# Four graph layers on one core: nodes without edges first, and their dense work beside the edges' tiles

## The chip, the core and the metric

The kernel runs on one core of one Trainium2 chip. The metric is the device time of one execution in microseconds (us). Five engines have programs of their own: TensorE (PE in the profile, its weight loads PEld), VectorE (DVE), ScalarE (ACT), GpSimd (POOL) and SyncE (SP), which only issues DMAs. They meet by semaphores.

## The reference, cut to what matters

There are 10000 nodes with rows of 512 f32, and 5000 edges (src, dst) with drawn ends, sorted by dst. So at least half of the nodes receive no edge.

```python
h = x + segment_sum(x[src], dst)                       # GIN
x = layernorm(x + relu(h @ W1 + b1) @ W2 + b2)

mean = segment_sum(x[src], dst) / max(count, 1)        # SAGE and batch norm
h = mean @ W_l.T + b_l + x @ W_r.T
x = layernorm(x + relu(batch_norm(h)) + x)

# GAT twice (4 heads of 256 columns, every node has a loop edge), then a dense layer
h1 = relu(gat_conv(x,  src+loop, dst+loop, W1, ...))   # softmax over a node's edges
h2 = relu(gat_conv(h1, src+loop, dst+loop, W2, ...))
x = layernorm(x + h2 @ Wfc + bfc)

xw = x @ W.T                                           # GCN and batch norm
h = segment_sum(norm[:, None] * xw[row], col) + b      # loops included
x = layernorm(x + gelu(batch_norm(h)) + x)
```

What counts for the change: a node without an edge takes nothing from another node. Its sum is zero, its softmax is the loop's own weight, 1, and its GCN row is its own row times its scale.

## The kernel before, in words

**Tiling.** Nodes lie in DRAM in 20 groups of 512 (`GROUP`), each of 4 subtiles (`S`) of 128 rows (`P`). Edges lie in 40 tiles of 128 (`T`). An edge stage gathers the source rows of a tile by one indirect DMA on POOL, multiplies them on PE by a 128x128 matrix that joins edges of one target, and stores the 128 sums in a table in DRAM (`sum`, or `sum_gat` with the attention's weights). Sums that cross a tile's edge are joined at the end, in "rim" rows. A node stage takes the sum of each of its nodes out of that table by an indirect DMA per subtile on POOL, through `slot_i` (`gather_sums`, L1639); nodes without an edge find a row of zeros. Products in f32 are made of three in f16, of high and low parts (`split_product`, L316 to L327).

**Stages.** The program is a list of stages. In each, every engine has its own list of work in a fixed order, written out by hand; no planner sets it. Between two stages there is a barrier (all engines drain and meet at a semaphore, in `Kernel.run`, L287 to L292). In order: setup (degrees, slots and masks of the edges) with the first edge sum; `gin_stage` (L1644); `edge_product_stage` (L1086: sums of the x1 rows times W_l); `sage_stage` (L1843); batch norm coefficients; `batch_norm_stage` (L2040, which also makes h1 = x W1 of the first attention with its score columns); `edge_attention_stage` for h1 (L1249); `gat_middle_stage` (L2298: sums, bias and ReLU, times W2, stores h2); `edge_attention_stage` for h2; `gat_stage` (L2483: sums, bias and ReLU, times Wfc, residual and norm, stores x3); `edge_sum_stage` over x3 (L975); `gcn_stage` (L2738); coefficients; `output_stage` (L2858).

**An attention tile.** POOL gathers a score row of the target and a full row (1028 values and more) of the source. DVE adds the scores (L1367) and leaks them, ACT spreads them to 128 columns, PE turns them into rows (L1543, a product with the identity), DVE masks them and takes the maximum (L1380, L1385) and subtracts it, ACT takes the exponential, PE sums the weights (L1552), DVE inverts (L1401) and makes four 128x128 matrices (`a_lhs`, L1414), PE multiplies them by the gathered rows (L1560), ACT evacuates the two banks and SP stores them. Most buffers of this chain, its PSUM banks too, are double or more.

**GIN.** Per group SP loads x, POOL gathers the sums and adds the bias (L1732), DVE and ACT make high and low parts, PE multiplies twice, POOL does a part of the norm (L1617), DVE applies it, and SP stores the group's 512 rows of x1 with one contiguous DMA (`store`, L1703). In `output_stage` POOL makes the norm's shift (L2908, L2911) and SP stores the group's output rows with one contiguous DMA (L2896).

**SAGE and GCN.** Per group SP loads the rows, POOL gathers sums, PE transposes both by 128x128 blocks (`tp`, L1986 and L2838) and multiplies them, columns of features being the partitions. SAGE's POOL also gathers 40 single scales of 4 bytes. `Held` (L2715) is the class that finds room in SBUF for the GCN rows that stay there until the output.

Of the kernel before, what the change touches and what calls it, by code (L numbers as in the profile page):

```python
# [5 lines left out]
F32 = mybir.dt.float32  # L6
# [7 lines left out]
P = 128  # L14
# [35 lines left out]
class Dims:  # L50
    def __init__(self, nodes, edges):
# [10 lines left out]
        self.slots = self.none + 1  # L62
        self.last_real = nodes - (self.groups - 1) * GROUP
        assert self.sent >= nodes and 0 < self.last_real <= GROUP
# [107 lines left out]
class Kernel:  # L172
    def __init__(self, nc, ctx, dims, dram):
# [25 lines left out]

        self.apart = sb("apart", [P, T, P], F16)  # L200
        self.dst_f = sb("dst_f", [P, T + 1], F32)
        self.src_i = sb("src_i", [P, T], I32)
        self.dst_logits_i = sb("dst_logits_i", [P, T], I32)
        self.src_dinv_i = sb("src_dinv_i", [P, T], I32)
        self.slot_i = sb("slot_i", [P, d.blocks], I32)
        self.mean_scale = sb("mean_scale", [P, T], F32)
        self.src_dinv = sb("src_dinv", [P, T], F32)
        self.src_dinv_neg = sb("src_dinv_neg", [P, T], F32)
        self.rim_mean_scale = sb("rim_mean_scale", [P, 1], F32)

        self.dst_dinv = sb("dst_dinv", [P, T], F32)
        self.rim_dinv = sb("rim_dinv", [P, 1], F32)
        self.node_scale = sb("node_scale", [P, d.blocks], F32)
        self.rim_cross = sb("rim_cross", [P, T], F32)
        self.rim_pen = sb("rim_pen", [P, T], F32)
        self.rim_tiles = sb("rim_tiles", [P, 1], F32)
        self.node_dinv = sb("node_dinv", [P, d.blocks], F32)
# [135 lines left out]
class Tables:  # L353


    def __init__(self, kn):
# [6 lines left out]
        self.degrees = take("target_degrees", 2)  # L363


def setup_stage(kn, mem, tables):
# [20 lines left out]
    blank = sb("blank", [1, HC], F32)  # L387
# [47 lines left out]
    off_first = sb("off_first", [P, T, T], F16)  # L435
# [13 lines left out]
    rim_count_ps = kn.bank[0][0:T, 0:1]  # L449

# [6 lines left out]
    consts = Steps(take("const_steps", 13))  # L457
# [4 lines left out]
    products = take("setup_products", 7)  # L462
    COUNTED, ROWS_SUMMED, BASED, TIED, SORTED_DONE, ENDS_DONE, RIM_COUNTED = range(1, 8)
# [3 lines left out]
    turned = take("turned", Q)  # L467
# [9 lines left out]
    edge_steps = Steps(take("edge_steps", 6))  # L477
# [4 lines left out]
    mask_steps = Steps(take("mask_steps", 12))  # L482
    slot_steps = Steps(take("slot_steps", 14))
# [14 lines left out]
    def sync_late(sp):  # L498
        sp.wait_ge(degrees.sem, degrees.at(2))
        sp.dma_start(dram["dinv"].rearrange("(p r) c -> p (r c)", p=P), kn.node_dinv[:]).then_inc(dinv_out.sem, 16)  # L500
        sp.wait_ge(dinv_out.sem, dinv_out.at(16))
        sp.wait_ge(tables.zeroed.sem, tables.zeroed.at(48))

    def gpsimd(pool):
# [5 lines left out]
        g.memset(blank[:], 0.0).then_inc(blank_ready.sem, 1)  # L510
# [6 lines left out]
        g.memset(kn.eps[:], EPS)  # L517
        b = st.mark(g.memset(kn.minus_half[:], -0.5))
# [13 lines left out]
        assert n == st.sig.at(13)  # L532

        pool.wait_ge(hist_ready.sem, hist_ready.at(1))
        g.tensor_scalar(degree[:], hist[:], 1.0, None, ALU.add).then_inc(degrees.sem, 1)
        pool.wait_ge(degrees.sem, degrees.at(1))
        g.tensor_tensor(kn.node_dinv[:], degree[:], kn.minus_half[:], ALU.pow).then_inc(degrees.sem, 1)

    def scalar(act):
# [3 lines left out]
        for c in range(Q):  # L543
            act.wait_ge(turned.sem, turned.at(c + 1))
            act.copy(high_turned[0:K, c * 4 * P:(c + 1) * 4 * P], wide_ps[c % 2][0:K, :]).then_inc(turned_ready.sem, 1)

    def vector(dve):
# [30 lines left out]
        dve.wait_ge(consts.sig.sem, consts.sig.at(13))  # L578
# [81 lines left out]
        dve.wait_ge(consts.sig.sem, consts.sig.at(13))  # L660
# [17 lines left out]
    def ends(dve):  # L678
# [10 lines left out]
        v.tensor_tensor(off_first[:], dst.unsqueeze(2).broadcast_to([P, T, T]),  # L689
# [11 lines left out]
    def finish(dve):  # L701
# [5 lines left out]
        st.mark(v.tensor_scalar(kn.dst_logits_i[:], kn.dst_f[:, 0:T], float(GAT_ROW // LOGITS), None, ALU.mult))  # L707
        edge_steps.mark(v.scalar_tensor_tensor(out=kn.src_dinv_i[:], in0=edge_f[:, :, 2], scalar=float(K),
                                               in1=edge_f[:, :, 0], op0=ALU.mult, op1=ALU.add))
# [2358 lines left out]
```

## Time and profile before

| what | value |
|---|---|
| median of 3 runs (lowest, highest) | 3914.8 us (3913.59, 3915.11) |
| profiled execution, time | 3912.85 us |
| profiled execution, span | 3911.1 us |
| mean granted TensorE clock over the span | 0.932 |
| PE busy | 3419.3 us, 87% of the span, 19416 matmuls |
| DVE busy | 2155.2 us, 55% |
| ACT busy | 1463.1 us, 37% |
| POOL busy | 1452.1 us, 37% |
| DMA | 821 MB, mean 210 GB/s |

The stages, read from the barriers in the trace:

| stretch, us | stage |
|---|---|
| 0 to 199.2 | setup and the first edge sum |
| 199.3 to 655.4 | GIN |
| 659.7 to 835 | edge products |
| 835.2 to 1128 | SAGE |
| 1137 to 1624.5 | batch norm and h1 |
| 1628 to 1812.5 | edge attention over h1 |
| 1812.9 to 2688.7 | middle attention stage |
| 2688.7 to 2873.5 | edge attention over h2 |
| 2873.8 to 3401.5 | second attention's nodes, dense layer |
| 3402.5 to 3495.8 | edge sum over x3 |
| 3495.8 to 3758 | GCN |
| 3763.6 to 3911.1 | output |

The span is the time from the first to the last record of the profiled execution; its own time is 1.75 us longer. Shares of busy time are means over stages with different limits, so each stage is read by itself. The granted clock is told as a share of full speed, 1.00 being 2.4 GHz. In a row, "128x512 f32<-128x344 f16" is the shape and type of what is written and read, and the text in brackets at the end of a row is the time in which the engine was idle ahead of it and what ended that.

### The profile page before, as it was taken

What the parts mean: (1) busy time and instruction counts of PE and PEld (TensorE: products, weight loads), DVE (VectorE), ACT (ScalarE), POOL (GpSimd) and SP (SyncE); (2) the same over time, 40 slices, a digit from 0 to 9 for tenths busy, and PEclk for the clock granted to TensorE, in tenths of its full rate; (3) what the DMA queues carried; (4) which work ended last, traced back from release to release, by engine and by line L of the source; (5) the groups of instructions that cost most, each with busy time, mean ns of one, the idle gap of its engine ahead of it and who ended that gap; (6) DMA issues with size and microseconds to landing.
All of it is one profiled execution on the core that took longest, in us unless ns stands there. A gap on an engine that the chain in (4) does not pass through costs nothing. (4 is left out here: it accounts for less than half of the span.)

```text
span 3911.1 us, 55988 instructions
## 1 busy us (share of the span) xinstructions
PE 3419.3 (87%) x19416; PEld 2074.1 (53%) x19416; DVE 2155.2 (55%) x3972; ACT 1463.1 (37%) x2580; POOL 1452.1 (37%) x1231
## 2 busy tenths in 40 slices
PE   4669998989969999886999999998859999859964
PEld 3234443545637666664666666666635555315543
DVE  7257775845554444276543443413758888406667
ACT  1323332533324444353332332322534444233357
POOL 2345553225422222253333323212536666343312
PEclk7789999989979999997999999999979999979976
DMA  2667774656659999597978878944957777375558
GB/s 82 201 184 198 196 201 146 201 172 228 227 195 259 279 274 281 180 280 213 256 192 204 204 194 198 200 119 146 280 209 259 262 261 262 123 231 186 174 167 275
DMA packets 624227, 821.41 MB, mean 210 GB/s; under 512 B 378374, under 2 KB 378374, under 8 KB 622032
## 3 DMA queue, kind: packets, MB, share of 16 engines
q1 hardware_dynamic: 556880, 598.37, 50.3%
q0 software_dynamic: 67200, 221.25, 20.1%
q8 instruction: 71, 1.16, 0.1%
q14 instruction: 76, 0.62, 0.1%
HBM read 470.83 MB, written 263.59 MB: 188 GB/s over the span
## 5 line engine op out<-in xcount | busy, mean ns | idle before, releaser
L326 PE MATMUL bank<-w_lo,t_r_hi 128*128 128x344 f16 (+1 forms) x2560 | 838.8, 328 | 0.0
L327 PE MATMUL bank<-w_hi,t_r_hi 128*128 128x344 f16 (+1 forms) x2560 | 838.6, 328 | 0.0
L325 PE MATMUL bank<-w_hi,w_lo 128*128 128x344 f16 (+1 forms) x2240 | 716.7, 320 | 49.8 <-DMA w_lo<-g_row_lo 31.3
L2415 DVE SCALAR_TENSOR_TENSOR t_z<-w_lo,t_z 128x256 f32<-128x256 f32 x320 | 243.5, 819 | 396.4 <-DMA w_lo<-h 393.4
L326 PE MATMUL bank<-w_lo,w_hi 128*128 128x344 f16 (+1 forms) x1280 | 419.6, 328 | 0.0
L327 PE MATMUL bank<-w_hi 128*128 128x344 f16 (+1 forms) x1280 | 419.4, 328 | 0.0
L2389 POOL TENSOR_TENSOR t_row_lo<-t_r,t_row_hi 128x1024 f16<-128x1024 f32 x80 | 174.9, 2187 | 509.8 <-ACT t_row_hi L2436 509.8
L327 PEld LDWEIGHTS bank<-w_hi,t_r_hi 128*128 128x128 f16 x2560 | 250.9, 98 | 168.8 <-issue 0.8
L326 PEld LDWEIGHTS bank<-w_lo,t_r_hi 128*128 128x128 f16 x2560 | 250.9, 98 | 162.5 <-issue 0.6
L325 PE MATMUL bank<-w_hi 128*128 128x344 f16 x960 | 298.3, 311 | 21.8 <-DMA w_hi<-t_row_lo 19.2
L325 PEld LDWEIGHTS bank<-w_hi,w_lo 128*128 128x128 f16 x2240 | 219.3, 98 | 181.7 <-issue 50.8
L325 PE MATMUL bank<-l_z_hi,w_lo 128*128 128x512 f16 x640 | 244.4, 382 | 1.4 <-DVE l_z_lo L2798 1.4
L326 PE MATMUL bank<-l_z_lo,w_hi 128*128 128x512 f16 x640 | 244.3, 382 | 0.0
L327 PE MATMUL bank<-l_z_hi,w_hi 128*128 128x512 f16 x640 | 244.1, 381 | 0.0
L325 PE MATMUL bank<-w_hi,t_r_lo 128*128 128x512 f16 x640 | 243.6, 381 | 0.0
L2591 POOL TENSOR_TENSOR t_r_lo<-t_r,t_r_hi 128x512 f16<-128x512 f32 x160 | 196.0, 1233 | 97.1 <-ACT t_r_hi L2659 90.1
L2447 ACT ACTIVATE w_hi<-bank 128x344 f32<-128x344 f32 x240 | 104.5, 454 | 339.5 <-PE bank L327 339.4
L2656 ACT ACTIVATE t_r<-bank,vec_scaled 128x512 f32<-128x512 f32 x160 | 109.6, 685 | 293.0 <-PE bank L2687 241.4
L1639 POOL DMA_INDIRECT t_z<-sum_gat,slot_i x160 | 163.0, 1019 | 122.0 <-SPq L292 79.1
L2243 ACT ACTIVATE b_wide<-bank 128x344 f32<-128x344 f32 x240 | 109.2, 456 | 253.1 <-PE bank L327 253.1
L1617 POOL TENSOR_TENSOR n_power<-n_moments,eps 128x4 f32<-128x4 f32 x80 | 15.9, 199 | 502.9 <-DVE n_moments L1611 502.9
L2622 DVE SCALAR_TENSOR_TENSOR t_z<-w_lo,t_z 128x256 f32<-128x256 f32 x320 | 187.0, 645 | 21.4 <-DMA t_z<-sum_gat,slot_i 13.3
(345 smaller groups left out, 6732.2 us busy)
## 6 DMA issues: line engine op xcount, KB each, us to landing
w_lo<-h SPq DMA_DIRECT2D x160, 512.0 KB, 5.7
h<-b_wide SPq DMA_DIRECT2D x80, 516.0 KB, 9.6
h<-w_hi SPq DMA_DIRECT2D x80, 516.0 KB, 2.9
sum_gat<-a_out SPq DMA_DIRECT2D x80, 514.0 KB
l_x<-x SPq DMA_DIRECT2D x40, 1024.0 KB, 9.1
sum<-e_out SPq DMA_DIRECT2D x120, 256.0 KB
g_x<-in_x SPq DMA_DIRECT2D x20, 1024.0 KB, 5.6
x<-g_y SPq DMA_DIRECT2D x20, 1024.0 KB, 5.1
```

The costliest lines, as they stand in the source:

```text
L325: pe.matmul(out, s_lo, m_hi, start=(k == 0), stop=False)
L326: pe.matmul(out, s_hi, m_lo, start=False, stop=False)
L327: mm = pe.matmul(out, s_hi, m_hi, start=False, stop=last)
L1617: self.nc.gpsimd.tensor_tensor(self.power[:, u, :], self.moments[:, u, :, 1], self.kn.eps[:], ALU.add)\
L1639: pool.indirect_dma_start(out, None, sums, bass.IndirectOffsetOnAxis(ap=kn.slot_i[:, g * S + s:g * S + s + 1], axis=0), bounds_check=kn.d. ...
L2243: act.activation(wide[s][:, n * THIRD:(n + 1) * THIRD], mm[n], ACT.Copy, scale=UNSCALE)\
L2389: nc.gpsimd.tensor_tensor(row_lo[:, s, :], r_f[s % 2][:], row_hi[:, s, :], ALU.subtract)\
L2415: ins = v.scalar_tensor_tensor(out=z[u][:, s, cols], in0=hrow[:, s, cols], scalar=z[u][:, s, HC + h:HC + h + 1], in1=z[u][:, s, cols], op0 ...
L2447: act.activation(wide[s % 2][:, third * THIRD:(third + 1) * THIRD], mm[s % 2][third], ACT.Copy, scale=UNSCALE).then_inc(wide_done.sem, 1)
L2591: g_.tensor_tensor(r_lo[:, u, k, :], r_f[k % 2][:], r_hi[:, u, k, :], ALU.subtract)\
L2622: ins = v.scalar_tensor_tensor(out=z[u][:, s, cols], in0=hrow[:, s, cols], scalar=z[u][:, s, HC + h:HC + h + 1], in1=z[u][:, s, cols], op0 ...
L2656: act.activation(r_f[k % 2][:], tp[k % 4][:], ACT.Relu, scale=A_SCALE, bias=kn.vec_scaled[:, bias + k:bias + k + 1]).then_inc(r_done.sem, 1)
```

## The change

**Order.** Setup also counts the nodes with no edge (`alone`), ranks them with two small products on PE, and gives every node a place: those without an edge first, the others behind them, each in their old order (`places_of_nodes`). `Dims.early` is the number of groups, a multiple of two, that are sure to hold only nodes without an edge: (10000 - 5000) // 1024 * 2. The input x keeps its order. `gin_stage` reads by nodes and stores x1 by places, with four indirect DMAs per group on POOL (`to_places`) in place of SP's one; all stages behind it work by places; `output_stage` stores by nodes again, with four indirect DMAs per group on POOL. A small DRAM table by node (scale and place) is read in GIN and SAGE, 40 times each, once per tile and end of the edges (`look_up`). A table by place (node, slot, scale) is written by 80 indirect DMAs on POOL in `edge_product_stage`, two per tile, and loaded by SP in `sage_stage`. There the `early` groups skip the gathers of sums, their transposes and the additions.

```diff
+        self.early = max(nodes - edges, 0) // (2 * GROUP) * 2
+def to_places(kn, pool, rows, g, s, landed):
+    pool.indirect_dma_start(kn.dram["x1"], bass.IndirectOffsetOnAxis(ap=kn.place_i[:, g * S + s:g * S + s + 1], axis=0),
+                            rows, None, bounds_check=kn.d.padded - 1, oob_is_err=False).then_inc(landed.sem, 16)
+def look_up(kn, pool, out, at, t, landed):
+    pool.indirect_dma_start(out[:, t, :], None, kn.dram["by_node"],
+                            bass.IndirectOffsetOnAxis(ap=at[:, t:t + 1], axis=0),
...
 def edge_product_stage
+        def store_by_place(k):
+            pool.indirect_dma_start(dram["by_place"], bass.IndirectOffsetOnAxis(ap=kn.place_at_i[:, k:k + 1], axis=0),
+                                    kn.by_place[:, k, :], None, ...)
...
 def gin_stage, gpsimd
             norm.pool(pool, *divmod(g, 2))
             if g + 3 < G:
                 load_sums(g + 3)
+            store(g)
+            for t in range(g * per, min((g + 1) * per, d.tiles)):
+                look_up(kn, pool, kn.src_by, kn.src_at_i, t, found)
...
 def sage_stage, gpsimd
+        pool.wait_ge(table_in.sem, table_in.at(16))
...
+        for t in range(T):
+            look_up(kn, pool, dst_by, kn.dst_at_i, t, found)
+        for g in range(E, G):
             load_sums(g)
...
 def output_stage, gpsimd
+            if g:
+                store(g - 1)
+        store(G - 1)
```

**Merged stages.** The work of an edge stage becomes a class with one method per engine and tile (`AttentionEdges`, `RowEdges`), and a new stage runs it beside the dense work of the first 8 groups. The edge steps are shared out evenly over the slots of that work: a slot is a third of a subtile's product in the first (96 slots for 45 steps), a subtile's product in the second and third (32 slots for 45 and for 41 steps). Each engine does a slot's dense work and then its edge steps, in a fixed order. Behind each stands the old node stage, now for the other 12 groups.

```diff
+def shared_out(steps, slots):
+    return [range(n * steps // slots, (n + 1) * steps // slots) for n in range(slots)]
...
+            for third in range(THIRDS):                  # gat_middle_early_stage, PE
+                pe.wait_ge(wide_done.sem, wide_done.at((j - 1) * THIRDS + third + 1))
+                split_product(pe, mm[third], ..., CH).then_inc(prod.sem, 1)
+                for e in steps[j * THIRDS + third]:
+                    edges.tensor_step(pe, e)
...
+            for s in range(S):                           # rows_product_early_stage, PE
+                if g + 1 < E:
+                    turn(g + 1, (2 * s, 2 * s + 1))
+                pe.wait_ge(y_done.sem, y_done.at(g * S + s - 1))
+                split_product(pe, mm[s % 2][:], ..., CH, hidden if s == 0 else None).then_inc(prod.sem, 1)
+                for e in steps[g * S + s]:
+                    edges.tensor_step(pe, e)
...
+    def tensor(self, pe, t):                             # AttentionEdges, one tile on PE
+        pe.wait_ge(self.lhs_ready.sem, self.lhs_ready.at(t + 1))
+        pe.wait_ge(self.evacuated.sem, self.evacuated.at(2 * t))
+        for h in range(HEADS):
+            ins = pe.matmul(...)
+        ins.then_inc(self.summed.sem, 1)
+        if t + 1 < self.T:
+            self.sum_weights(pe, t + 1)
+        if t + 2 < self.T:
+            self.score_rows(pe, t + 2)
+    def vector(self, dve, t):                            # and on DVE, as vector_step(dve, t - 1)
+        self.matrices(dve, t)
+        if t + 1 < self.T:
+            self.maxima(dve, t + 1)
...
-        kn.add(edge_attention_stage(kn, dram["h1"]))
+        kn.add(gat_middle_early_stage(kn))
         kn.add(gat_middle_stage(kn))
-        kn.add(edge_attention_stage(kn, dram["h2"]))
+        kn.add(rows_product_early_stage(kn))
         kn.add(gat_stage(kn, 2))
         with ExitStack() as mem:
-            kn.add(edge_sum_stage(kn, mem, dram["x3"], (kn.src_dinv, kn.src_dinv_neg), kn.dst_dinv, kn.rim_dinv))
-        with ExitStack() as mem:
             held = Held(kn, mem)
+            kn.add(gcn_early_stage(kn, held))
             kn.add(gcn_stage(kn, held))
```

To fit beside the dense work, `AttentionEdges` keeps 4 gathered tiles (6 before) and 3 outputs (4 before), and single buffers for the masked scores and `a_lhs`, and single banks for the totals, the score rows and the weights' sums. The score rows are now turned by `pe.transpose` in place of a product with the identity. In `gat_middle_early_stage` DVE makes `z * A_SCALE + bias` and the low part of 1024 columns for each subtile, ACT the high part, and both parts are transposed by DMAs from SP. In `rows_product_early_stage` the rows of h2 are transposed on PE, ACT makes ReLU and the high part of each of 8 chunks of 512 columns per group, and POOL the low part, behind whose first group the edges' first four tiles of gathers stand. `gcn_early_stage` keeps the edges' buffers in rows of `Held` that the GCN stage fills only later.

## Rows read from the trace of the kernel before

**Rows 1.** Stretches: stages. Columns: window, length, five engines busy, clock, DMA share, GB/s.

```profile
835.20:1128.00 292.80, 282.24 (x1600) 168.97 (x1600) 157.66 (x241) 94.34 (x160) 127.51 (x124) 0.97 0.63 212
1628.00:1812.50 184.50, 143.87 (x748) 111.26 (x748) 122.94 (x462) 84.12 (x201) 79.79 (x80) 0.92 0.78 233
1812.90:2688.70 875.80, 847.35 (x5776) 567.60 (x5776) 343.81 (x402) 259.92 (x401) 254.92 (x160) 0.98 0.79 192
2873.80:3401.50 527.70, 489.73 (x2560) 262.61 (x2560) 388.05 (x640) 202.87 (x320) 303.52 (x280) 0.96 0.65 239
3402.50:3495.80 93.30, 54.16 (x82) 16.85 (x82) 1.16 (x2) 42.51 (x80) 39.99 (x40) 0.79 0.72 228
```

**Rows 2.** Stretches: slices of 50 us inside the two attention node stages.

```profile
2000.00:2050.00 50.00, 50.00 (x345) 33.55 (x343) 20.93 (x25) 14.23 (x22) 13.86 (x9) 1.00 0.80 191
3000.00:3050.00 50.00, 50.00 (x265) 26.68 (x264) 40.74 (x67) 20.96 (x34) 31.74 (x30) 1.00 0.72 266
```

**Rows 3.** Order of instructions, PE and DVE, attention tile: start, us, engine, line.

```profile
1700.26 2.00 PE L1560 MATMUL bank<-a_rows,a_lhs 128*128 128x256 f32 x8 [0.42 <-DVE a_lhs L1414]
...
1702.53 1.14 PE L1543 MATMUL bank<-ident,a_spread 128*128 128x128 f32 x8
1704.09 2.00 PE L1560 MATMUL bank<-a_rows,a_lhs 128*128 128x256 f32 x8 [0.43 <-DVE a_lhs L1414]
...
1703.35 0.69 DVE L1414 SCALAR_TENSOR_TENSOR a_lhs<-apart,a_out 128x512 f32<-128x512 f16 x1
```

**Rows 4.** Order of instructions, PE, second attention's node stage: twelve transposes.

```profile
3008.65 1.47 PE L2687 MATMUL bank<-ident,t_z 128*128 128x128 f32 x12
3009.96 0.38 PE L325 MATMUL bank<-w_hi,t_r_lo 128*128 128x512 f16 x1
```

**Rows 5.** Line L325, PE: count, ns min/median/max, first and last start, us.

```profile
L325 PE MATMUL bank<-w_hi x960: 308/309/495, 1837.0 to 2642.1; 128*128 128x344 f16 x192
L325 PE MATMUL bank<-l_z_hi,w_lo x640: 378/379/635, 849.1 to 3756.9; 128*128 128x512 f16 x160
L325 PE MATMUL bank<-w_hi,t_r_lo x640: 378/379/632, 2911.5 to 3391.9; 128*128 128x512 f16 x160
L325 PE MATMUL bank<-w_hi,e_z_lo x160: 378/379/390, 674.5 to 826.0; 128*128 128x512 f16 x160
```

**Rows 6.** Groups by line: count | busy, mean | idle before, its end.

```profile
L2591 POOL TENSOR_TENSOR t_r_lo<-t_r,t_r_hi 128x512 f16<-128x512 f32 x160 | 196.0, 1233 | 97.1 <-ACT t_r_hi L2659 90.1
L1639 POOL DMA_INDIRECT g_z<-sum,slot_i x80 | 110.4, 1381 | 42.6 <-issue 21.9 <-SPq L292 20.5
L1639 POOL DMA_INDIRECT l_a<-sum,slot_i x80 | 79.7, 997 | 173.8 <-PE bank L1986 114.8 <-SPq L292 38.7 <-issue 20.3
L1130 POOL DMA_INDIRECT e_rows<-x,src_i x40 | 45.5, 1138 | 98.6 <-PE bank L1215 86.2 <-POOLq L292 7.4 <-issue 5.0
```

**Rows 7.** Order of instructions, PE, edge products: one tile's sum.

```profile
677.10 1.02 PE L1215 MATMUL bank<-e_rows,e_lhs 128*128 128x512 f32 x2
```

**Rows 8.** Order of instructions, POOL, one group of GIN.

```profile
419.36 0.20 POOL L1617 TENSOR_TENSOR n_power<-n_moments,eps 128x4 f32<-128x4 f32 x1 [5.13 <-DVE n_moments L1611]
...
422.60 2.10 POOL L1639 DMA_INDIRECT g_z<-sum,slot_i  x1 [0.30 <-issue]
...
426.40 1.08 POOL L1639 DMA_INDIRECT g_z<-sum,slot_i  x1 [0.30 <-issue]
430.67 4.53 POOL L1732 TENSOR_TENSOR g_y<-g_x,gin_b 128x2048 f32<-128x2048 f32 x1 [3.19 <-DVE g_row_lo L1758]
440.47 0.20 POOL L1617 TENSOR_TENSOR n_power<-n_moments,eps 128x4 f32<-128x4 f32 x1 [5.26 <-DVE n_moments L1611]
```

**Rows 9.** Order of instructions, POOL, one group of the output stage.

```profile
3822.32 0.20 POOL L1617 TENSOR_TENSOR n_power<-n_moments,eps 128x4 f32<-128x4 f32 x1 [4.67 <-DVE n_moments L1611]
...
3824.00 0.23 POOL L2911 TENSOR_SCALAR o_shift<-o_shift 128x4 f32<-128x4 f32 x1
3828.90 0.20 POOL L1617 TENSOR_TENSOR n_power<-n_moments,eps 128x4 f32<-128x4 f32 x1 [4.67 <-DVE n_moments L1611]
```

More of the change, by code:

```diff
@@ L363, in __init__ @@
         self.degrees = take("target_degrees", 2)
+        self.places = take("places_known", 2)
 def setup_stage(kn, mem, tables):
@@ L806, in tensor @@
             ins.then_inc(looked_up.sem, 1)
+        pe.wait_ge(alone_steps.sig.sem, alone_steps.sig.at(3))
+        pe.wait_ge(table_ready.sem, table_ready.at(B))
+        pe.matmul(alone_total_ps, alone[:], kn.ones[:], start=True, stop=True).then_inc(products.sem, 1)
         pe.wait_ge(ties_ready.sem, ties_ready.at(B))
@@ L812, in tensor @@
         ins.then_inc(products.sem, 1)
+        pe.wait_ge(ranked.sem, ranked.at(1))
+        pe.matmul(ranks_ps[:, 0:K], above, alone[:], start=True, stop=False)
+        pe.matmul(ranks_ps[:, 0:K], alone_total[0:K, :], above[0:K, 0:K], start=False, stop=True)
+        pe.matmul(ranks_ps[:, K:K + 1], alone_total[0:K, :], kn.ones[0:K, 0:1], start=True, stop=True)\
+            .then_inc(products.sem, 1)
         pe.wait_ge(table_ready.sem, table_ready.at(B))
@@ L1133, in gpsimd @@
                 .then_inc(gathered[t % W].sem, 16)
+            for k in range(t * per, min((t + 1) * per, d.blocks)):
+                store_by_place(k)
+        pool.wait_ge(table_out.sem, table_out.at(16 * d.blocks))
     def sync(sp):
@@ L1668, in gin_stage @@
     x_in = pair("x_in", 16 * H)
-    sum_in = pair("sum_in", 16 * S * H, software=True)
+    sum_in = [take(f"sum_in{u}_0", 16 * S * H, software=True) for u in range(2)]
     z_ready = pair("z_ready", H * S)
@@ L1681, in gin_stage @@
     rows_out = pair("rows_out", S * H)
-    stored = pair("stored", 16 * H)
+    placed = pair("placed_out", 16 * S * H, software=True)
+    found = take("dinv_in", 16 * d.tiles, software=True)
+    sources = take("sources_ready", 1)
     def sync(sp):
@@ L1710, in sync @@
                 load_x(g + 2)
-            if g:
-                store(g - 1)
             if g + 1 < G:
                 turn(g + 1)
-        store(G - 1)
-        for u in range(2):
-            sp.wait_ge(stored[u].sem, stored[u].at(16 * H))
     def gpsimd(pool):
@@ L2767, in sync @@
     def sync(sp):
-        for g in range(G):
+        for g in range(N):
             i, u = divmod(g, 2)
@@ L2821, in scalar @@
         high_parts(0)
-        for g in range(G):
+        for g in range(N):
             for m in range(4):
-                if g + 1 < G and m == 1:
+                if g + 1 < N and m == 1:
                     high_parts(g + 1)
-                own = held.rows[g][m]
+                own = held.rows[E + g][m]
                 act.wait_ge(mid.sem, mid.at(g * 4 + m + 1))
@@ L2841, in tensor @@
         turn(0)
-        for g in range(G):
+        for g in range(N):
             u = g % 2
@@ L2845, in tensor @@
             for m in range(4):
-                if g + 1 < G and m == 1:
+                if g + 1 < N and m == 1:
                     turn(g + 1)
@@ L2894, in sync, with store @@
                 load(g + B)
[L2895 to L2901 removed]
+    def gpsimd(pool):
+        def store(g):
+            pool.wait_ge(rows_out.sem, rows_out.at(g * S + S))
+            for s in range(S):
+                pool.indirect_dma_start(dram["out"],
+                                        bass.IndirectOffsetOnAxis(ap=kn.node_i[:, g * S + s:g * S + s + 1], axis=0),
+                                        x[g][:, s, :], None, bounds_check=d.padded - 1, oob_is_err=False)\
+                    .then_inc((first_stored if g < B else stored).sem, 16)
         for g in range(G):
```

1418 lines of the change are left out of this document (1009 added, 409 removed).

## The prediction

> **What bounds the kernel now.** I read the stretches of the stages first, then even slices inside them, then the order of instructions. The program is a chain of stages with a barrier between any two, so each stage adds its own time. The ones that matter here stand in [rows 1]. In the node stages PE is the bound: in a slice of 50 us it is busy for all 50 at a granted clock of 1.00 (the 2.4 GHz level), with 345 matmuls of 344 columns in the middle attention stage (0.145 us each) and 265 instructions in the last attention stage [rows 2]. The reader is to see the contrast with the two edge attention stages (184.5 us, and 2873.8 - 2688.7 = 185 for the second, between the rows beside it) and the edge sum stage (93.3 us): there no node is worked on, PE shows 144 us busy in the first, and much of that is waiting for a chain. One tile of 128 edges takes 3.83 us (products at 1700.26 and again at 1704.09), in which DVE, ACT and PE take turns and PE's products wait 0.43 us for DVE's a_lhs although they had been free before [rows 3]. What the change can win is this idle time of PE.
>
> "Early" comes out of Dims: (10000 - 5000) // 1024 * 2 = 8 groups of 20. Tiles: 40.
>
> **First merged stage (gat_middle_early_stage).** PE's own work adds. Dense: 8 groups x 288 matmuls x 0.145 = 334 us. A tile's PE work: eight product instructions and the weights' sum, 2.14 (2.27 lie between the start of the products and that of the score rows [rows 3]; I take 0.13 of it for the wait for ACT), and the score rows, which were 8 instructions with 1.14 and are now 4 transposes. Twelve such transposes take 1.31 us from their start to the next matmul, 0.109 each [rows 4], so 0.44. Sum 2.6, for 40 tiles 104 us, and about 4 for the rims. 45 edge steps fall on 96 slots of 3.5 us, so there are about 10 us between two steps, against 3.83 for a whole chain: it hides. DVE gets the new bias and low part, about 2.8 us per subtile (an estimate: two operations of twice 512 columns, at the 0.69 of a_lhs's 512 [rows 3]). With 32 subtiles at 2.8, the edge stage's 123 and 8/20 of the middle stage's 344 [rows 1] it is busy for 350 of 480 us and fits. DMA fits too: 0.78 x 184.5 = 144 us of full use, and 0.79 x 876 / 20 = 35 per group, 8 of them 277, before the gathers that go: under 421 of 480. Fill: I take the 24 us that the middle stage needs from 1812.9 to its first product at 1837.0 [rows 1, 5]. Tail 4, stalls 10. Sum 24 + 334 + 104 + 4 + 4 + 10 = 480. Removed: 184.5 and 8 groups at (2688.7 - 4 - 1837.0) / 20 = 42.4, together 524. **Gain 44.**
>
> **Second merged stage (rows_product_early_stage).** Dense per group: 96 matmuls of 512 columns. From the slice of 265: 50 us hold 265 instructions of which a quarter are transposes at 0.109, so a matmul is (50 - 66 x 0.109) / 199 = 0.215; 96 x 0.215 + 32 x 0.109 = 24.2, which agrees with (3393 - 2911.5) / 20 = 24.1. Eight: 194. Tiles 104, rims 4. Here 45 steps fall on 32 slots, so 13 slots hold two. In such a slot the second product waits for DVE's matrices, and DVE's maxima and ACT's weight (both now on single buffers) come after: I follow it as 6.75 us for 5.2 of work, 13 x 1.6 = 21. Fill: POOL issues 8 gathers first (1.3 each, 10 us), then the low parts, 1.23 each [rows 6], then ACT starts the edges: 25. Tail 10 (last norm and store). Sum 358, against 185 + 193 = 378. **Gain 20.** With no stall it would be 41; if each of the 80 tiles of both stages kept its 3.83, it is a rival below.
>
> **Third merged stage (gcn_early_stage).** Per group 4 x (12 x 0.215 + 0.44) = 12.1, eight 97. A tile here is one product of two instructions on 512 columns of f32, 1.02 with the end of the pipeline [rows 7]; as four times 0.215 for a matmul of 512 columns in f16 it is 0.86 of issue, and 40 are 35. Lhs and PSUM are double or better, so two steps in a slot do not stall. Fill as in the SAGE stage, which has the same shape, 849.1 - 835.2 = 14 [rows 1, 5]; tail 14, because the last tile falls in the last slot and its rim rows must land, which the stage before paid too. 160, against 93.3 + 97 = 190. **Gain 30.**
>
> **SAGE stage.** Eight groups lose 16 transposes each: 8 x 16 x 0.109 = 14. PE is the bound there, but a group is then (1128 - 849.1) / 20 - 1.74 = 12.2 us, and the load of 1 MB per group and the store of 1 MB get less time: I keep 12. POOL gets 40 lookups before the first gather (52 us), hidden before group 8 at about 98 us. Its new wait is the small table behind two loads: what is queued behind it, the gathers of group 8, has slack.
>
> The removed gathers, DVE combinations and scale steps of eight groups lie beside PE: worth nothing in themselves. The last two node stages keep 12 groups and their own fills.
>
> Gains: 44 + 20 + 30 + 12 = **106**.
>
> **What it adds: POOL.** The order by places makes x1 and the output scatters on POOL's queue, four per group, in place of one store of SP. None is in the trace. The nearest rows are the indirect gathers of as many rows: 1.0 us in the mean in the SAGE stage [rows 6] with 0.30 between two, and from 1.08 to 2.10 in the GIN stage [rows 8]; both are my ends.
> GIN stage: one group takes 21.1 us (norm at 419.36 and at 440.47). POOL: norm and gathers end at 427.48, 8.1 in; four scatters at 1.08 + 0.3 make 13.6; two lookups 16.3; add_bias, 4.53, makes 21.0. That is the period itself, with nothing left. Behind the norm is DVE's apply and with it PE's next operand. I charge 0.3 x 20 = **6**; with 2.10 it would be 88.
> Edge product stage: a gather has mean 1.138 there [rows 6], and two scatters of 12-byte rows per tile follow it: 3 x 1.14 + 0.9 = 4.1 to 4.3 us against PE's (826.0 - 674.5) / 39 = 3.9 per tile [rows 5]. The gathers run ahead of their use (86 us of their idle time is waiting for banks that PE still uses [rows 6]) and spend that lead: **7** (0 to 15).
> Output stage: one group takes 6.58 us (3822.32 to 3828.90) and POOL 1.9 of them. Four scatters, 5.2, make 7.1 to 7.3: POOL becomes the bound. 19 x 0.65 = 12, and the last group is stored after the one before it by 5.2 + 5.2 in place of SP's store: 5. **17** (15 to 100) [rows 9].
> Setup: one small matmul before the ties, 0.6, the rest beside DVE: **1**. The wider tables and the order of the nodes cost nothing else; loads stay contiguous.
>
> In the GIN stage the slow gathers stand behind DVE's four scalings between SBUF tiles; one took 2.10, one 1.08 [rows 8]. By the Trainium skill, SBUF — State Buffer, section "SBUF: two separate sides", a DMA issued on GpSimd waits for its descriptors while DVE holds the shared port, and one issued on SP does not: it speaks against moving the stores. By that rule, if all scatters met such operations, they would be near the 2.10 end; the trace shows 1.0 where DVE works from PSUM.
>
> **Sum:** 106 - 31 = 75. The profiled execution took 3912.85 (span 3911.1 and 1.75 around it), so 3838; the median of the runs shown is 2 us above it: **3840 us**.
>
> **Rivals.** A. Scatters longer. There are 240 on POOL in three stages that it then bounds, so each 0.1 us costs 24 us; the gain is gone at 0.31 us more, a mean of 1.35, and the mean of the gathers in the GIN stage is just 1.38 [rows 6]. With 1.5 the time is 3840 + 0.45 x 240 = 3948, **slower**. Against it: most would fall where DVE reads PSUM. 0.16. This is also the port rule of the page above as a mechanism here.
> B. The chains do not hide: PE, in order, waits 3.83 in each of 80 tiles. 80 x 1.23 = 98, less the 21 charged: 3917, no change. For it: single buffers and four engines in fixed order; against it: 10 us between steps in the first merged stage. 0.09.
> C. All hidden: no stalls (10 + 21 less) and POOL a bound in the output stage alone (6 + 7 less): 3840 - 44 = 3796. 0.13.
> The forecast, 3810 to 3870: 0.62.
> Faster by more than 0.2% (what the runs tell from no change): 0.62 + 0.13 + 0.02 for the fast edge of B, 0.77. Same 0.05, the middle of B. Slower 0.18: A, and 0.02 of B. The range, 3795 to 3895, leaves out A, half of B and the far side of C, some 2 in 10.
>
> **What would show it.** The three merged stages should last about 480, 358 and 160 us; PE near fully busy with few idle times before the edge products in the first, and in the second waits for a_lhs and a_weight in 13 slots. SAGE should take about 281. POOL should be almost without idle time in GIN and output, with groups at 21.1 to 21.5 and 7.1 to 7.3 us. It is wrong if a scatter takes clearly more than 1.1 us, if dense products wait for r_lo, transposed rows or evacuations, or if the merged stages' fills pass 30 us.

## The result: 0.4% slower

The changed kernel took 3932.4 us (median of 17 runs, 3919.7 to 3945.3) against 3914.6 us before (17 runs, 3910.5 to 3926.7): 1.0042 of the time before, 95% interval 1.0031 to 1.0053. The forecast was 3840, range 3795 to 3895. The measured time lies outside the range and on the other side of no change. The profiled execution has a span of 3930.5 us.

The stretches of the changed kernel's stages: window, length, busy time and count of PE, PEld, DVE, ACT and POOL, granted clock, DMA share, GB/s. In order GIN, edge products, SAGE, first merged stage and its node stage, second and its node stage, third and its node stage, output.

```profile
200.90:694.90 494.00, 422.94 (x1920) 185.24 (x1920) 316.57 (x560) 148.85 (x241) 349.96 (x261) 0.95 0.64 170
694.90:909.80 214.90, 173.26 (x722) 84.13 (x722) 119.34 (x112) 81.87 (x160) 145.42 (x120) 0.89 0.49 159
909.80:1238.10 328.30, 276.45 (x1472) 156.37 (x1472) 135.82 (x210) 94.72 (x160) 96.55 (x95) 0.90 0.52 167
1734.60:2194.10 459.50, 436.82 (x2892) 315.60 (x2892) 198.02 (x528) 155.65 (x331) 82.81 (x80) 0.97 0.80 204
2194.10:2734.90 540.80, 512.37 (x3472) 342.96 (x3472) 205.99 (x242) 156.85 (x241) 155.41 (x96) 0.97 0.77 187
2734.90:3099.60 364.70, 310.39 (x1604) 198.57 (x1604) 222.35 (x590) 163.91 (x329) 165.85 (x160) 0.94 0.65 210
3099.60:3434.10 334.50, 295.40 (x1536) 159.33 (x1536) 231.21 (x384) 121.70 (x193) 182.68 (x168) 0.94 0.62 226
3434.10:3585.20 151.10, 136.43 (x594) 69.75 (x594) 45.50 (x66) 80.10 (x144) 39.97 (x40) 0.94 0.61 197
3585.20:3753.10 167.90, 149.44 (x768) 79.64 (x768) 92.56 (x144) 56.84 (x96) 49.04 (x48) 0.93 0.54 151
3757.70:3929.80 172.10, 68.12 (x320) 61.33 (x320) 118.02 (x240) 115.06 (x160) 113.39 (x160) 0.62 0.73 244
```

Read against [rows 1], and summed from barrier to barrier in us:

| stages | before | after | gain | forecast |
|---|---|---|---|---|
| setup, first sum | 194.4 | 196.1 | -1.7 | -1 |
| GIN | 460.6 | 494.0 | -33.4 | -6 |
| edge products | 175.5 | 214.9 | -39.4 | -7 |
| SAGE | 296.7 | 328.3 | -31.6 | +12 |
| batch norm, h1 | 490.5 | 492.0 | -1.5 | 0 |
| first merge and its nodes | 1060.8 | 1000.3 | +60.5 | +44 |
| second | 714.5 | 699.2 | +15.3 | +20 |
| third | 356.5 | 319.1 | +37.4 | +30 |
| output | 147.1 | 172.1 | -25.0 | -17 |

So the merged stages gave 113 us, 19 more than forecast. The stages that pay for the new order (setup, GIN, edge products, SAGE, output) cost 131, where I had 31 less the 12 that SAGE was to gain.

In the second merged stage PE waits where I said. A slot with two edge steps, in order of start, us:

```profile
2855.91 1.99 PE L1701 MATMUL bank<-a_rows,a_lhs 128*128 128x256 f32 x8
...
2860.56 1.99 PE L1701 MATMUL bank<-a_rows,a_lhs 128*128 128x256 f32 x8 [1.74 <-DVE a_lhs L1522]
```

and PE's waits over that stage (us in total, times, longest) say that this is the main one:

```profile
PE bank L1701 <- DVE a_lhs L1522: 21.8, 10, 6.4
PE bank L3102 <- DMA w_lo<-h: 12.1, 1, 12.1
```

Only eight of the ten waits, of 0.9 to 1.7 us, are of the kind that I had counted, each in a slot with two edge steps. The two long ones, 6.4 and 5.1 us, have another cause: DVE works in order, and it stands ahead of its edge work until a row block of the residual has been loaded. The first of them, on DVE:

```profile
2892.52 0.69 DVE L3046 SCALAR_TENSOR_TENSOR w_hi<-bank,w_hi 128x512 f32<-128x512 f32 x1 [6.99 <-DMA w_hi<-x_biased]
```

**SAGE stands still.** POOL issues its block of 40 look-ups from 919.7 to 971.5, one in 1.30 us. PE goes on until 936.7, stands still for 11 us, works for 6 us, and then runs one instruction in 2.1 to 2.8 us until 972.5; it takes up its work again at 983.1, behind the block and the eight gathers of sums that POOL issues next. ACT and DVE nearly stop with it. The DMA engines are all but idle while the block lasts, and busy behind it (slices of 15 us, columns as above):

```profile
925.00:940.00 15.00, 11.72 (x55) 5.72 (x53) 2.67 (x4) 2.46 (x4) 11.63 (x12) 0.92 0.06 2
940.00:955.00 15.00, 6.22 (x25) 3.21 (x25) 1.39 (x2) 1.28 (x2) 11.35 (x13) 0.66 0.04 1
955.00:970.00 15.00, 3.39 (x7) 0.61 (x6) 0.00 (x0) 0.00 (x0) 11.65 (x12) 0.61 0.05 1
970.00:985.00 15.00, 1.92 (x6) 0.82 (x5) 1.39 (x2) 1.28 (x2) 9.19 (x10) 0.50 0.86 233
...
1000.00:1015.00 15.00, 15.00 (x82) 8.15 (x80) 6.29 (x11) 5.87 (x10) 0.00 (x0) 1.00 0.63 211
```

Some of PE's instructions in it (start, us; in brackets the idle time before it; "issue" means that nothing in the profile released it). The last three belong to one product:

```profile
936.34 0.38 PE L350 MATMUL bank<-l_z_hi,w_hi 128*128 128x512 f16 x1
947.96 1.12 PE L2249 MATMUL bank<-ident,l_x 128*128 128x128 f32 x4 [11.23 <-issue]
...
959.86 0.59 PE L348 MATMUL bank<-l_z_hi,w_lo 128*128 128x512 f16 x1 [2.42 <-issue]
961.96 0.58 PE L349 MATMUL bank<-l_z_lo,w_hi 128*128 128x512 f16 x1 [1.52 <-issue]
964.76 0.58 PE L350 MATMUL bank<-l_z_hi,w_hi 128*128 128x512 f16 x1 [2.22 <-issue]
```

### The profile page after: what moved, and what is told of

The parts are those of the page before. It is cut to its first block and busy times, and to the rows that moved or that the text cites. A ratio compares the mean times of both kernels' runs of the same rounds, so it can differ in the third digit from the quotient of the medians.

```text
span 3930.5 us, 54418 instructions
## 1 busy us (share of the span) xinstructions
PE 3348.5 (85%) x18968; PEld 2028.7 (52%) x18968; DVE 1998.9 (51%) x3698; ACT 1430.8 (36%) x2551; POOL 1564.7 (40%) x1359
## 5 line engine op out<-in xcount | busy, mean ns | idle before, releaser
L348 PE MATMUL bank<-w_hi 128*128 128x344 f16 (+1 forms) x1216 | 396.6, 326 | 27.2 <-DMA w_hi<-t_row_lo 20.5
L350 PE MATMUL bank<-w_hi 128*128 128x344 f16 (+1 forms) x1280 | 419.8, 328 | 0.0
L1439 POOL DMA_INDIRECT a_own<-h,edge_tables x80 | 81.9, 1023 | 543.2 <-PE bank L1701 383.6
L2875 DVE SCALAR_TENSOR_TENSOR t_z<-w_lo,t_z 128x256 f32<-128x256 f32 x192 | 146.7, 822 | 200.4 <-DMA w_lo<-h 197.3
L2849 POOL TENSOR_TENSOR t_row_lo<-t_r,t_row_hi 128x1024 f16<-128x1024 f32 x48 | 106.4, 2217 | 283.4 <-ACT t_row_hi L2896 283.4
L1701 PE MATMUL bank<-a_rows,a_lhs 128*128 128x256 f32 x640 | 157.4, 390 | 24.0 <-DVE a_lhs L1522 21.8
L348 PEld LDWEIGHTS bank<-w_hi 128*128 128x128 f16 x1216 | 119.9, 99 | 101.4 <-issue 24.8
L350 PEld LDWEIGHTS bank<-w_hi 128*128 128x128 f16 x1280 | 125.7, 98 | 84.8 <-issue 1.0
L349 PEld LDWEIGHTS bank<-w_lo,w_hi 128*128 128x128 f16 x1280 | 125.8, 98 | 82.0 <-issue 0.8
L2433 POOL TENSOR_TENSOR b_o<-b_o,fc_b 128x2048 f32<-128x2048 f32 x20 | 90.5, 4523 | 149.1 <-DVE b_row_lo L2469 149.1
L2058 ACT ACTIVATE g_r<-bank,vec_scaled 128x512 f32<-128x512 f32 x80 | 54.3, 678 | 259.2 <-PE bank L350 255.5
```

The source lines that it names most:

```text
L348: pe.matmul(out, s_lo, m_hi, start=(k == 0), stop=False)
L349: pe.matmul(out, s_hi, m_lo, start=False, stop=False)
L350: mm = pe.matmul(out, s_hi, m_hi, start=False, stop=last)
L1439: pool.indirect_dma_start(self.own[w][:], None, self.logits_dram, bass.IndirectOffsetOnAxis(ap=kn.dst_logits_i[:, t:t + 1], axis=0), bound ...
L1701: ins = pe.matmul(self.total[h // 2][:, (h % 2) * C:(h % 2 + 1) * C], self.lhs[:, h, :], self.rows[w][:, LOGITS + h * C:LOGITS + (h + 1) * ...
L2058: act.activation(r_f[m % 2][:], mid_ps[m][:], ACT.Relu, scale=GIN_UNSCALE * GIN_SCALE, bias=kn.vec_scaled[:, V_GIN_B1 + m:V_GIN_B1 + m + 1 ...
```

## The experiments

All edits are made to the changed kernel. Times are medians of the runs given, the ratio, with its 95% interval in brackets, is to the kernel before on the same chip, and the times of stages are from the profiled execution. Runs 1 to 4 share a chip, 5 to 8 another, 9 and the first of 10 a third, the rest of 10 and 12 a fourth, 11 and 13 a fifth. "Stand-still" is what the rows above show.

**1. The merged stages alone.** x1 and the output by SP in whole groups, no table, no look-ups in GIN; the pieces of the diff that make the order by places are undone.

> The merged stages alone: x1 and the output stored by SP in whole groups, the order of the nodes kept, no table by place, 40 look-ups spread over SAGE as in the kernel before (left out: the order by places, so nodes with edges in the first 8 groups get no sum). Theory 1 (the merged stages give 60 + 15 + 37 = 113 us and the order's traffic on POOL takes 131): GIN 461, edge products 176, SAGE about 285, output 147, the three merged pairs 1000, 699 and 319 as in the changed kernel; total about 3787. Rival (the merged stages gain by something that the order brings, or the stages lose by code size or layout): the total is above 3830.

3779.5 us (4 runs), 0.9661 (0.9645 to 0.9677). GIN 461.3, edge products 176.2, SAGE 280.7, output 147.7; the three merges 993.6, 701.1, 316.2. The theory holds to 8 us: the order by places, not the merging, is what costs.

**2. The look-ups of SAGE spread.**

```diff
-        for t in range(T):
-            look_up(kn, pool, dst_by, kn.dst_at_i, t, found)
+        per = -(-T // (G - E - 2))
         for g in range(E, G):
             load_sums(g)
+            for t in range((g - E - 1) * per, min((g - E) * per, T)) if g > E else ():
+                look_up(kn, pool, dst_by, kn.dst_at_i, t, found)
```

> The changed kernel, but the 40 look-ups of SAGE (8-byte rows) no longer stand in one block ahead of the first gather of sums; they are issued four at a time between the gathers of the last groups, which PE's progress paces. Theory 1 (the block of small look-ups itself holds up the other engines, which stood still for 11 us and then ran one instruction per 2 to 3 us between 936 and 983 in the changed kernel): the SAGE stage goes from 328 to about 285 us, total 3932 to about 3889. Rival (the stall comes from something else that falls in this stretch, such as the loads of instructions or the stage's start): SAGE stays near 328 and the total near 3932.

3875.0 us (4 runs), 0.9909 (0.9892 to 0.9925). SAGE 281.9, as theory 1 said; the edge products, which the edit doesn't touch, took 204.7 instead of 214.9. That was the first sign that something besides the text differs.

**3. Full rows in the place of the look-ups.** A block of 40 gathers of x1 rows (`dram["x1"]`, 2048 bytes each) into SAGE's `a` buffers, five in flight; the look-ups spread as in 2.

> As the kernel with the look-ups spread, but with 40 gathers of full rows (2048 bytes, values that nobody uses) in the place where the block of look-ups was: the same number of POOL issues at the same 1.30 us. Theory 1a (it is the rows of 8 bytes): no instruction-by-instruction stall of PE, SAGE at 285 to 295 us, the rest contention for bandwidth. Theory 1b (it is POOL issuing software DMAs without a pause, whatever the row): the stall is there again, SAGE at about 328 us.

3883.8 us (4 runs), 0.9921 (0.9900 to 0.9942), SAGE 288.7.

**4. No table by place.**

```diff
-            for k in range(t * per, min((t + 1) * per, d.blocks)):
-                store_by_place(k)
...
-        sp.dma_start(kn.by_place[:], dram["by_place"]...)
```

> The changed kernel without the table by place: none of the 80 scatters of 12-byte rows in the edge product stage, no load of the table in SAGE (left out: slots and node numbers are then those of the order of nodes, so the rows that are gathered and the places of the output differ, not their count or size). Theory 1 (the scatters cost both POOL's time, 4.9 us per tile against PE's 3.9, and stalls of PE, ACT and DVE between 760 and 885): the edge product stage goes from 215 to about 177 us, total to about 3893. Rival (the stage is longer because its source rows now lie by place or because of what GIN's scatters leave behind): it stays above 200.

3844.8 us (4 runs), 0.9828 (0.9812 to 0.9845). Edge products 175.6: the scatters are the whole cost there. But SAGE took 280.6 with its block of look-ups untouched: on this chip the block did no harm. A slice inside its block, in which PE is busy throughout:

```profile
902.00:917.00 15.00, 15.00 (x81) 8.12 (x79) 6.42 (x10) 5.73 (x11) 11.53 (x12) 1.00 0.63 194
```

So 2 to 4, run together, could not say what brings the stand-still, and that theory 1 of experiment 2 hit its number was luck: nothing stood still on this chip.

**5. POOL's order in GIN.** Two of the four gathers of sums moved behind the scatters.

```diff
-                load_sums(g + 3)
+                load_sums(g + 3, range(2))
             store(g)
+            if g + 3 < G:
+                load_sums(g + 3, range(2, S))
```

> The kernel with the look-ups of SAGE spread, and in GIN only the order of POOL's queue changed: of the four gathers of sums that stand ahead of a group's four scatters, two now stand behind them, so that more lies between the last scatter and add_bias, which waits for the scatters to land (they share its buffer). Theory 1 (GIN is 35 us longer because POOL waits 2.2 us per group for the landing on top of its 20.5 us of work): that wait is gone, a group takes 21 us as before, GIN goes from 496 to about 463 us, total from 3875 to about 3842. Rival (GIN is bound by POOL's issues as such, or by contention of the scatters with the transposing DMAs): GIN stays above 485.

3879.8 us (4 runs), 0.9910 (0.9892 to 0.9927), GIN 496.4. POOL's wait for the landing is gone from its list of waits, and GIN did not get shorter: theory 1 falls. PE still waits 18 us in all for `w_lo<-g_row_lo`.

**6. Rows of 512 bytes in the edge products.** `dram["wide"]` of 128 columns takes the 80 scatters, from `ident`.

> Look-ups of SAGE spread; the 80 scatters of 12-byte rows in the edge product stage write rows of 512 bytes to another DRAM tensor instead, at the same count and place, and the table by place is left out (as in the run without it). Theory 1 (small rows stall the other engines and POOL itself): with rows of 512 bytes POOL takes its 3 x 1.3 = 3.9 to 4.1 us per tile and nothing stalls, so the stage takes 180 to 188 us, between the 176 without scatters and the 205 to 215 with small rows. Rival (POOL's issue time alone makes it longer): it takes 200 or more, as with the small rows.

3872.3 us (4 runs), 0.9900 (0.9878 to 0.9921), edge products 204.4, as with 12 bytes (204.7 in 2, 207.3 in 5). The rival holds: it is the number of POOL's issues and not the size of their rows. The Trainium skill, DMA: Bandwidth & Descriptors, section "Specifications", puts the smallest transfer at full rate at 512 bytes and says that a DMA engine reads, modifies and writes below it. Whatever that does to the transfers, it did not set this time.

**7. Half of the table in SAGE.** One scatter per tile stays in the edge products; the other 40 stand at the head of SAGE's POOL queue, each behind `pool.wait_ge(turned.sem, turned.at((k - T) // 2 + 1))`, and SP loads the table before group 5's store. With edit 2.

> Look-ups of SAGE spread, and only half of the table's scatters (one per tile) in the edge product stage; the other 40 stand at the head of SAGE on POOL, two for every four transposes of PE, and the table is loaded before the sixth group. Theory 1: POOL has slack in both stages (2.6 us per tile against 3.9; 10 us per group of 12), so edge products take about 178 us and SAGE about 282: total from 3875 to about 3849. Rival (it is the number of small rows in flight, paced or not, that stalls the engines): the time lost moves with the scatters, edge products near 190 and SAGE near 295, total near 3875.

3850.4 us (4 runs), 0.9838 (0.9822 to 0.9855): edge products 175.6, SAGE 286.3, 4.4 more than without them. Theory 1 holds.

**8. Edits 2, 5 and 7 together.**

> The three edits together (look-ups spread, half of the table in SAGE, GIN's POOL queue reordered). If the terms add: 3932 - 57 - 26 - 33 = about 3816. If they share a cause, more than that.

3852.8 us (4 runs), 0.9842 (0.9819 to 0.9865): 5 brings nothing, as it did alone (GIN 497.5).

**9. GIN without look-ups, and without scatters,** each with edits 2 and 7.

> The kernel with half of the table in SAGE and all look-ups there; GIN has its 80 scatters and no look-up (left out: src_i stays by nodes in the edge product stage; the 40 look-ups stand in SAGE among the others). Without them GIN takes 496, its groups 22.2 us with PE waiting 0.9 us per group for the transposed low part, whose DMA takes 4.5 us in place of 2.5, and its end 14 us more than before. Theory 2 (the look-ups' 128 small rows fall on the low part's transposing DMA): groups at 21.1 to 21.3, GIN at about 474 (461, end 11 longer). Rival (it is the four scatters of 512 rows of 2048 bytes): GIN stays at 490 or more.

> The kernel with half of the table in SAGE; in GIN x1 is stored by SP in whole groups as in the kernel before (left out: x1's order by places) and the 40 look-ups stay. Theory 2 (the look-ups delay the transposing DMA): groups stay at 22 us and GIN at about 485, only the end gets shorter. Rival (the scatters do): groups at 21.1 us, GIN at about 466.

Without look-ups 3854.7 us (4 runs), 0.9851 (0.9834 to 0.9867), GIN 491.8; without scatters 3819.1 (4 runs), 0.9757 (0.9741 to 0.9773), GIN 462.6 and every group at 21.1 or 21.2 us. So it is the scatters. (SAGE, with 80 look-ups in the run without them, took 296.0, which hides the gain of GIN in its total.) What they do is seen on the DMA that transposes the next group's low part (count: ns min/median/max, first and last start). Before:

```profile
L1697 SPq DMA_TRANSPOSE w_lo<-g_row_lo x20: 1820/2556/3250, 220.9 to 622.1; - x20
```

the changed kernel:

```profile
L1951 SPq DMA_TRANSPOSE w_lo<-g_row_lo x20: 2677/4477/4958, 222.2 to 643.0; - x20
```

without look-ups, and without scatters:

```profile
L1948 SPq DMA_TRANSPOSE w_lo<-g_row_lo x20: 2502/4398/4711, 222.1 to 647.6; - x20
```

```profile
L1950 SPq DMA_TRANSPOSE w_lo<-g_row_lo x20: 1618/2644/4265, 222.2 to 624.0; - x20
```

Without scatters SP stores the group at an earlier time and in one DMA, so whether their kind or their time slows the transposing DMA is not told apart.

**10. The changed kernel again.**

> The changed kernel as it is, for a second profile. Theory 1 (the stand-still of PE, ACT and DVE comes of a fixed cause in SAGE): again one of about 45 us between the start of SAGE and its first gathers, SAGE near 328 us. Rival (it can strike anywhere while POOL issues small rows without a pause): the stretches move, between the edge product stage and SAGE, with the same sum of 50 to 60 us over the 382 that the two take without it... that is edge products plus SAGE near 543 in both profiles against 487 in the run with the look-ups spread.

3885.2 us (one run; before 3914.1, 7 runs): SAGE 287.0, edge products 205.6, no stand-still. Theory 1 and the rival both fall. The same text, on another chip:

> The changed kernel as it is, timed again: 17 runs gave 3919.7 to 3945.3, and a single later one 3885.2, without the stand-still of 46 us in SAGE. Theory 3 (the stand-still comes and goes with where the program runs, not with its text): all six runs here lie on one side, either near 3885 or above 3919. Rival (it comes by chance from one execution to the next): runs of both kinds.

3935.9 us (6 runs, 3926.6 to 3943.0), 1.0052 (1.0036 to 1.0069), SAGE 329.8. All six lie on one side, as theory 3 says; the other side rests on the one run on the chip before. On that chip with edit 2:

> The kernel with the look-ups of SAGE spread, on the same chip as the changed one. If the block of look-ups costs nothing where nothing stands still: 5 us faster than the changed kernel at most (SAGE 282 against 287), near 3877. If spreading the look-ups is what removes the stand-still: 45 us or more faster.

3897.0 us (7 runs), 0.9960 (0.9945 to 0.9975), SAGE 290.8, 39 less; edge products 219.0, with gaps on ACT and DVE.

**11. What brings it, on a chip that shows it.**

> The changed kernel as it is, to tell whether this chip is one on which the stand-still occurs: near 3935 with SAGE at 329 us if it is, near 3885 with SAGE at 287 if not.

3936.9 us (3 runs), 1.0055 (1.0035 to 1.0074), SAGE 328.0: it is such a chip.

> The changed kernel without the table by place (left out, as before), the block of 40 look-ups in SAGE kept. On a chip with the stand-still: theory 4 (the block of look-ups alone brings it) gives SAGE near 325 us and the total near 3890; rival (it needs the scatters of small rows ahead of it) gives SAGE near 281 and the total near 3845, as measured on another chip.

3893.3 us (3 runs), 0.9944 (0.9925 to 0.9964), SAGE 328.0, edge products 174.8. The block alone brings the stand-still. The same text took 3842.6 to 3848.5 us in its 4 runs in experiment 4 and 3887.6 to 3894.3 in its 3 here, with SAGE at 280.6 and 328.0: it is not the text that decides. Each of these chips was used at one time only, so the chip is not told apart from the occasion. Its SAGE in slices of 15 us:

```profile
885.00:900.00 15.00, 12.77 (x54) 5.95 (x53) 1.87 (x3) 1.17 (x2) 11.45 (x12) 0.86 0.13 36
900.00:915.00 15.00, 1.93 (x4) 0.30 (x3) 0.75 (x2) 1.28 (x2) 11.47 (x12) 0.59 0.04 1
915.00:930.00 15.00, 0.00 (x0) 0.00 (x0) 0.64 (x1) 0.00 (x0) 11.53 (x12) 0.50 0.21 53
```

> The changed kernel with 40 gathers of rows of 2048 bytes in place of the block of look-ups, which are spread. On a chip with the stand-still: theory 4a (rows of 8 bytes bring it) gives SAGE near 290 us; theory 4b (any block of POOL's DMAs without a pause) gives SAGE near 325.

3893.9 us (5 runs), 0.9956 (0.9935 to 0.9976), SAGE 289.6. With rows of 2048 bytes, POOL busy for 8 to 11 us of 15 and the DMA engines for 78 to 92%, PE goes on:

```profile
929.00:944.00 15.00, 15.00 (x74) 7.65 (x73) 4.91 (x8) 4.41 (x8) 10.96 (x12) 0.93 0.78 250
944.00:959.00 15.00, 12.36 (x64) 6.34 (x63) 6.08 (x10) 5.30 (x9) 8.86 (x10) 1.00 0.87 299
959.00:974.00 15.00, 14.78 (x79) 7.93 (x78) 6.21 (x10) 6.10 (x10) 8.01 (x9) 1.00 0.92 311
```

So it is the block of 8-byte look-ups, issued without a wait, on some chips. In this run at most five gathers were in flight at a time, while nothing held the look-ups back, so the pacing is not told apart from the size of the rows.

**12. The shift of the output's norm on DVE,** with edits 2 and 7.

```diff
-            nc.gpsimd.tensor_tensor(shift[:, u, :], norm.moments[:, u, :, 0], norm.power[:, u, :], ALU.mult)
-            nc.gpsimd.tensor_scalar(shift[:, u, :], shift[:, u, :], -1.0, None, ALU.mult)
+            v.scalar_tensor_tensor(out=shift[:, g % 2, :], in0=norm.moments[:, g % 2, :, 0], scalar=-1.0,
+                                   in1=norm.power[:, g % 2, :], op0=ALU.mult, op1=ALU.mult)
```

> Look-ups spread, half of the table in SAGE, and in the output stage the two operations of the norm's shift taken off POOL's queue and made one of DVE. POOL has 7.36 us per group there, of which the shift takes about 1.2, and a group took 6.58 before. Theory: the stage goes from 172 to about 158 us and the total from 3850 to about 3836. Rival (DVE's wait for POOL's power or ACT's later start makes the group as long as before): 172 us, 3850.

3848.2 us (5 runs), 0.9825 (0.9812 to 0.9838), output 159.5: the term is right. The total is 12 above the expectation. This chip is one with the stand-still, and edge products took 181.0 and SAGE 296.6 on it (175.6 and 286.3 in 7), which is more than the difference; why they are longer here without the block is not shown.

**13. And GIN's look-ups off its end.**

```diff
-            for t in range(g * per, min((g + 1) * per, d.tiles)):
+            for t in range(g * d.tiles // (G - 1), min((g + 1) * d.tiles // (G - 1), d.tiles)):
```

> The kernel with the look-ups of SAGE spread, half of the table in SAGE and the shift on DVE (3848 where measured), and in addition GIN's 40 look-ups shared out over its first 19 groups, so that none stands behind the last group's scatters: 2.6 us less in GIN's end and a wait of 2.4 us for the last look-up that has landed by then; GIN from 497 to about 492, total about 3843.

3845.4 us (3 runs), 0.9817 (0.9798 to 0.9837), GIN 493.8. This version is 1.8% faster than the kernel before, on the chip where the changed kernel is 0.55% slower.

## Why the prediction was wrong

**The merged stages: right in kind.** First: the stage took 459 us for 480: fill 22.8 us (24), waits of PE 3.3 in place of 10, the rest of its work 12 shorter than summed; gain 60 for 44. Second: 13 double slots were to cost 21 us by waits for `a_lhs`. They were 21.8, but that the sum fits is partly luck: eight waits of the forecast kind make 10.2 us, and the other 11.6 are DVE's two waits for the residual's load, which I had not in the sum. Its stage took 365 for 358, the gain 15 for 20. Third: 151 for 160. Rival B, chains that do not hide, was wrong.

**Output: right in kind, short by 8.** POOL became the bound with 7.36 us per group for the 7.1 to 7.3 of the text, as its norm's first operation shows (the same form as [rows 9]):

```profile
3842.83 0.23 POOL L1857 TENSOR_TENSOR n_power<-n_moments,eps 128x4 f32<-128x4 f32 x1
...
3850.19 0.23 POOL L1857 TENSOR_TENSOR n_power<-n_moments,eps 128x4 f32<-128x4 f32 x1
```

The 19 groups cost 15 us where I had 12. Behind the last scatter POOL's drain at the barrier, 6.6 us, now ends the stage; it was not in my 5 for the end. SP's drain, which stood behind the store before, took 0.01.

**The length of a scatter: right.** "1.08 + 0.3" each; they took 1.05 in GIN, 1.00 in the output and 1.19 in the edge products, where rival A asked for a mean of 1.35 and more. Groups by line of the changed kernel (count | busy, mean ns | idle before):

```profile
L1886 POOL DMA_INDIRECT x<-g_y,place_i x80 | 84.0, 1050 | 31.8 <-issue 23.5 <-DVE g_y L1868 8.3
...
L1219 POOL DMA_INDIRECT by_place<-place_table,place_at_i x80 | 95.5, 1194 | 24.4 <-issue 23.5 <-PE bank L1314 0.6 <-remote 0.3
L1226 POOL DMA_INDIRECT e_rows<-x,edge_tables x40 | 49.9, 1247 | 26.5 <-issue 11.0 <-POOLq L315 9.1 <-remote 5.7
```

Had all of GIN's scatters met the shared port of the Trainium skill, SBUF — State Buffer, section "SBUF: two separate sides", I had them near the 2.10 of the slow gather; at 1.05 in the mean they did not. The outcome that A named, slower than before, came by other ways.

**GIN, "I charge 0.3 x 20 = 6": wrong, 33.** I asked only whether POOL's queue fits. It does, and removing its wait (5) changed nothing. Two things were left out. The scatters land while SP transposes the next group's low part, whose DMA goes from 2.56 to 4.48 us, and PE, without other work, waits about 1 us per group: PE's part of the stage grew by 19 us. SP's store had gone out 7.5 us ahead of the transposes; POOL's scatters, behind norm and gathers, fall on them. And the end, from PE's last product to the barrier, grew by 14.5, from 9.8 to 24.3: the last scatters, two look-ups, their landing, the cast (over at 686.6) and then POOL's drain, 8.3 us, stand in series there.

**Edge products, "7 (0 to 15)": mis-sized, 39, and 29 to 30 where nothing stood still.** Issues at 1.24 us in the mean (run of edit 2) and 0.30 between them make 4.6 us per tile, not 4.1 to 4.3: 40 of them 185 us, and POOL's last issue moved from 136 to 185 us into the stage. And I let the gathers' lead be spent whole. PE's last product comes 10 us behind the last issue, so only 20 of the 30 us of lead were there. Another 7 to 14 come on chips with the stand-still (212.0 to 219.0 in place of 204.7); by what is not shown.

**SAGE, "hidden before group 8": the largest miss, 44.** Hidden it was: without the stand-still the stage takes 281 to 287, near my 285 (296.7 less 12). The step that failed is "hidden": I took it that a block on a queue with slack costs the other engines nothing. On some chips it nearly stops them, from 936 to 983 us, and the stage takes 328, 41 more than the same text on a chip without it. There the changed kernel is faster than before by 29 us (3885 in the single run of 10), inside the range although 45 above the forecast, with the other misses as above. So this step sets the sign of the result, and no row of the trace before showed it, because there such look-ups come three at a time.

## What to carry to other kernels

Where work moves to another queue, count three things: whether it fits, what it now falls together with on the DMA side, and what it adds in series at the stage's end. Pace small indirect DMAs by another engine's progress rather than issue them in a block. And repeat a surprising result on another chip before explaining it: one text was 0.5% slower on two chips and 0.7% faster, in a single run, on a third.

## What the runs showed of the hardware

On two chips, in the profiles of the changed kernel and by their times in all its 9 runs there (and in the first 17), a block of 40 indirect DMAs of 128 rows of 8 bytes nearly stopped PE, ACT and DVE for about 47 us, with PE busy for 11 of them and for a part of them at one instruction in 2.1 to 2.8 us. The DMA engines were 4 to 6% busy from 925 to the end of the block, and POOL went on at 1.30 us per issue. The granted clock was 0.92 in the first of the slices above and 0.66, 0.61 and 0.50 (the 1.2 GHz level) in the next three, in which PE was busy for 6.2, 3.4 and 1.9 of 15 us. On a third chip, in one run, the same text did not, nor did the block alone on a fourth. Forty gathers of 2048-byte rows in the same place did not, on either of two chips, one of which showed it otherwise. What it is that PE waits for stays open: the profile names no releaser. That the engines' own instructions come late is a rival that no run tests; the two loads of instructions that the trace has in the stretch (at 929.1 and 964.8) took 1.4 and 0.4 us.
